# A Perceiver-like stack on one core: how the two mixtures of experts open, and where their router products and block list are made

## The reference, cut to what matters

```
x += cross attention over 8192 context rows, padded by a mask      (L0x)
x += self attention, keys j >= i only                              (L0a)
x += mixture: 8 experts, hidden size 2048, silu, top 2             (L0f)
x += cross attention over the context, masked by rows and columns  (L1x)
x += self attention in a window of 64 keys                         (L1a)
x += mixture: 8 experts, hidden size 1024, relu squared, top 2     (L1f)
```

```python
logits = xf @ router
top_v, top_i = jax.lax.top_k(logits, TOP_K)
w = jax.nn.softmax(top_v, axis=-1)
gates = jnp.sum(jax.nn.one_hot(top_i, E, dtype=x.dtype) * w[..., None], axis=1)
for e in range(E):
    h = xf @ W1[e]
    h = h * jax.nn.sigmoid(h)
    out = out + gates[:, e:e + 1] * (h @ W2[e])
```

## Time and profile before

| | us |
|---|---|
| median of 3 runs | 1856.64 (1856.35 to 1856.89) |
| profiled execution | 1861.01 |
| its span, first to last instruction | 1859.2 |
| TensorE busy | 1628.2 (88%) |
| VectorE busy | 1025.4 (55%) |
| ScalarE busy | 529.0 (28%) |
| GpSimd busy | 99.2 (5%) |
| mean granted clock of TensorE | 0.928 |

### The profile page before, as it was taken

How to read it: one execution, slowest core, us unless ns; L and a number is a source line. 1 busy time by engine, 2 the same in 40 slices (tenths; PEclk the granted TensorE clock), 3 DMA queues, 4 the chain that set the end, 5 groups by cost and what they waited for, 6 DMA issues and landing times. The chain is left out here.

```text
span 1859.2 us, 27460 instructions
## 1 busy us (share of the span) xinstructions
PE 1628.2 (88%) x9315; PEld 748.2 (40%) x9327; DVE 1025.4 (55%) x1655; ACT 529.0 (28%) x775; POOL 99.2 (5%) x82
## 2 busy tenths in 40 slices
PE   4899997999898949999999699997899898849994
PEld 1333322222233347765565233332222234447773
DVE  3577766999745521111111589996799735522222
ACT  1333423788413301111111111113578312200000
POOL 0100000200001010000001200002000001010001
PEclk9999978999998959999999799988999998969997
DMA  3424443221046367666661312315221020048995
GB/s 134 157 81 154 159 152 117 75 58 34 0 142 120 52 269 262 237 237 221 236 231 47 118 65 106 113 45 187 59 80 34 0 80 30 32 161 323 320 331 171
DMA packets 81010, 252.36 MB, mean 136 GB/s; under 512 B 7808, under 2 KB 25232, under 8 KB 60976
## 3 DMA queue, kind: packets, MB, share of 16 engines
q1 hardware_dynamic: 75120, 237.33, 38.2%
q0 software_dynamic: 2560, 8.39, 1.4%
q10 hardware_dynamic: 3264, 5.77, 0.8%
HBM read 223.68 MB, written 38.27 MB: 141 GB/s over the span
## 5 line engine op out<-in xcount | busy, mean ns | idle before, releaser
L1375 ACT ACTIVATE BIG<-banks 128x1024 f32<-128x1024 f32 (+5 forms) x320 | 282.0, 933 | 123.8 <-PE banks L1310 123.8
L937 DVE CUSTOM_DVE_ANT_0 BIG<-banks,MASK,MX 128x512 bf16<-128x512 f32 (+5 forms) x384 | 229.2, 656 | 75.8 <-PE banks L604 38.1
L1763 PEld LDWEIGHTS banks<-KF,BIG 128*128 128x128 f32 x1792 | 231.7, 194 | 13.7 <-issue 13.7
L1763 PE MATMUL banks<-KF,BIG 128*128 128x160 f32 (+1 forms) x1792 | 233.9, 293 | 2.0 <-DVE KF L1586 2.0
L604 PE MATMUL banks<-KF,XN 32*128 32x512 f32 (+4 forms) x1280 | 200.8, 635 | 18.8 <-DVE MX L937 9.4
L1780 PE MATMUL banks<-BIG,PB 128*128 128x512 f32 x448 | 202.8, 600 | 0.0
L1307 PE MATMUL banks<-XN,KF 32*128 32x512 f32 (+4 forms) x1280 | 174.2, 615 | 23.3 <-ACT BIG L1375 7.8
L1425 DVE TENSOR_TENSOR PB<-PB,BIG 128x2048 f32<-128x2048 f32 (+5 forms) x78 | 166.9, 2139 | 33.9 <-ACT BIG L1375 29.6
L930 DVE TENSOR_REDUCE MXW<-banks 128x2 f32<-128x1024 f32 x128 | 150.4, 1217 | 55.5 <-PE banks L615 54.7
L579 PE MATMUL banks<-WV,XNT 128*128 128x512 f32 x320 | 164.6, 636 | 0.0
L1277 PE MATMUL banks<-BIG,V 128*32 128x512 f32 (+4 forms) x1280 | 159.9, 568 | 2.9 <-ACT BIG L1375 2.8
(11 more groups left out here) (259 smaller groups left out, 1416.8 us busy)
## 6 DMA issues: line engine op xcount, KB each, us to landing
BIG<-in_L0f_w SPq DMA_DIRECT2D x64, 1024.0 KB, 4.7
BIG<-in_L1f_w SPq DMA_DIRECT2D x48, 1024.0 KB, 5.4
BIG<-in_mask_q SPq DMA_DIRECT2D x16, 1024.0 KB, 9.1
CT<-in_ctx SPq DMA_DIRECT2D x9, 1024.0 KB, 4.8
XNT<-in_ctx SPq DMA_DIRECT2D x9, 1024.0 KB, 5.9
k_saved<-KF SPq DMA_DIRECT2D x32, 256.0 KB, 2.7
v_saved<-V SPq DMA_DIRECT2D x32, 256.0 KB, 2.4
KF<-k_saved SPq DMA_DIRECT2D x32, 256.0 KB, 3.4
```

The source lines that it names most:

```text
L937: last = v.tensor_tensor_reduce(m.JUNK[:, 2 * half + e, k0:k1], pair[:, e, k0:k1], bias, 1.0, mx, ALU.add, ALU.max, mx)
L1375: a.activation(m.PE_[:, s % NP, 2 * half:2 * half + 2, q0:q1], m.pair[(2 * s + half) % 3][:, :, q0:q1], ACT.Exp).then_inc(exp_ready, 1)
L1763: last = t.matmul(out, W1[k][:, d, f * P:(f + 1) * P], XE[:, d, :], start=d == 0, stop=d == DC - 1)
```

## The change

- `project_out` of the two self attentions makes the router's logits itself, tile by tile, in bank 5: `logits(q)` stands after the output products of tile q + 2, the last two after the transposes of tiles 2 and 3. The mixture no longer makes them.
- Ranks: four products instead of ten. One covers the four tiles with the triangular weights, three add the earlier tiles to all later ones at once (the moving operand is repeated).
- Rows of rounds 0 and 1: VectorE makes a one-hot matrix HOT (tokens by slots, RS columns for each of four tiles) for experts 0 and 1 by comparing the rank with a ramp; TensorE multiplies XN by it (`hot_rows`), 16 products each, straight into the banks where the transposes would put them. Round 0's come right after the ranks, round 1's in round 0 in place of the transposes. HBM is read from round 2 on. The constant `rows` moves next to `ramp` so that the ramp can be 160 wide.
- The loads of rows move from SyncE to ScalarE, where they stand between the activations and the output copy of a round, under a conditional, behind a wait for the whole scatter and one for the transposes.
- TensorE's loop body has two conditionals more, `If(i < 1)` and `If(i >= 1)`. The number of rounds is written earlier (`counted`), and TensorE and ScalarE wait for that instead of the full list.
- The block list of L1x moves into the `row_maxima` of L0a: on TensorE after the first keys and queries, before the first scores, with a wait for its end; on VectorE ahead of the maxima.

```diff
@@ class Attention / row_maxima
+    U = unmasked_blocks(nc, m, n + "_blocks", m.UNMASKED[:, :, :], L.lists) if L.lists is not None else None
             if not dyn:
                 all_keys(0, [0])
                 all_queries(0)
+                if U:
+                    U.tensor(pe)
+                    pe.wait_ge(U.listed, U.listed_at)
                 pe.wait_ge(wv_loaded, 16)
                 scores(0, False)
...
             if not dyn:
                 dve.wait_ge(steps_done, 2)
+                if U:
+                    U.vector(dve)
                 maxima(0, False)
@@ project_out, tensor
+            def logits(q):
+                if router_loaded is None:
+                    return
+                pe.wait_ge(copied, q + 1)
+                for d in range(DC):
+                    last = t.matmul(m.bank[OUT[0]][:, E * q:E * q + E], m.XNT[:, d, q * P:(q + 1) * P], m.WR[:, d, :],
+                                    start=d == 0, stop=d == DC - 1)
+                last.then_inc(logits_done, 1)
...
                 last.then_inc(output_ready, 1)
+                if q > 1:
+                    logits(q - 2)
                 if q:
                     turn(q - 1)
+            logits(NQ - 2)
             turn(NQ - 1)
+            logits(NQ - 1)
@@ mixture, vector
-            dve.wait_ge(products_done, 1)
-            do(v.tensor_copy(LG, m.bank[0][:, 0:32]))
+            do(v.tensor_copy(LG, m.bank[5][:, 0:32]))
...
+            def one_hot(e):
+                for q in range(NQ):
+                    do(v.tensor_scalar(HOT[:, e, q, :], m.wide_ramp[:, 0:RS], RK[:, E * q + e:E * q + e + 1],
+                                       SM[:, E * q + e:E * q + e + 1], ALU.is_equal, ALU.mult))
+            one_hot(0)
+            m.mark["hot"] = m.steps
+            dve.wait_ge(products_done, 2)
+            do(v.tensor_scalar(m.CTL[0:1, C_NR:C_NR + 1], m.bank[3][0:1, 16:17], float(E), None, ALU.add))
+            m.mark["counted"] = m.steps
             do(v.tensor_scalar(CU, m.bank[3][0:E, 0:1], float(E), None, ALU.add))
             do(v.tensor_scalar(LE, m.ramp[0:E, 0:16], CU, None, ALU.is_ge))
             m.mark["of_round"] = m.steps
+            one_hot(1)
+            m.mark["hot1"] = m.steps
...
             m.mark["slots"] = m.steps
+            dve.wait_ge(transposed, 1 + B)
+            v.tensor_copy(XE[:, :, :].rearrange("p (a c) n -> p a (c n)", a=2), tokens).then_inc(tokens_copied, 1)
@@ mixture, sync: load_rows and its waits removed; the loads for L1x stand right behind W2
@@ mixture, scalar, after the activations of a round
+                    with act.If(i + 1 < nr):
+                        act.wait_ge(scattered, 2 * NQ * 16)
+                        wait_alone(act, transposed, i + 2 + B)
+                        act.dma_start(ROWS, XS[bass.ds(at + 2, 1), 0:P, :]...).then_inc(rows_loaded, 16)
@@ mixture, tensor
+            t.matmul(m.bank[7][:, 0:NQ * E], m.before[:, :], SM, start=True, stop=False, skip_group_check=True)
+            for b in range(NQ - 1):
+                last = t.matmul(m.bank[7][:, E * (b + 1):NQ * E].rearrange("p (t e) -> p t e", e=E), m.ones[:, :],
+                                r3(SM)[:, b:b + 1, :].to_broadcast([P, NQ - 1 - b, E]), start=False, stop=b == NQ - 2,
+                                skip_group_check=True)
...
+            def hot_rows(e):
+                for d in range(DC):
+                    out = tokens[:, d // 2, (d % 2) * RS:(d % 2) * RS + RS]
+                    for q in range(NQ):
+                        last = t.matmul(out, m.XN[:, q, d * P:(d + 1) * P], HOT[:, e, q, :], start=q == 0, stop=q == NQ - 1)
+                last.then_inc(transposed, 1)
+            pe.wait_ge(steps_done, m.mark["hot"])
+            hot_rows(0)
...
-                    transposes(i + 1)
+                    with pe.If(i < 1):
+                        pe.wait_ge(steps_done, m.mark["hot1"])
+                        hot_rows(1)
+                    with pe.If(i >= 1):
+                        transposes(i + 1)
```

93 lines of the change are left out of this document (39 added, 54 removed).

## The result

The changed kernel takes 1835.7 us (median of 4 runs, 1831.1 to 1837.0), the kernel before in the same comparison 1856.7 (1856.35 to 1856.89): ratio 0.988, 95% interval 0.9865 to 0.990, about 21 us faster. Forecast were 1823.2 us in a range of 1817 to 1832. The sign was right; of the 33.4 us forecast some 12 did not come. There the kernel before itself spread from 1849.6 to 1863.8 us in 23 runs, so a few microseconds between two medians of six runs say little, and what follows goes by the places in the traces as much as by the times.

What follows compares the result with a forecast made beforehand. TensorE was taken to bound the rounds, one serial path through several engines and DMA the mixtures' openings. Mixtures -22.4 and -20.8, attention ends +5.6, list +4.2 made -33.4 us: 1856.6 to 1823.2 us, range 1817 to 1832.

Steps and rivals of the forecast that it cites:

- Openings: Both mixtures, start to first hidden product: 16.05 us against 38.2 (-22.1) and 16.0 against 37.6 (-21.6).
- Clock in round 0 and rows of round 1: Mixtures: round 0 at high clock -2.9 and -2.3 us; round 1's row products on TensorE's path +2.6 and +3.1.
- Mixtures as a whole: Opening, round 0 clock and round 1 rows summed: first mixture -22.4 us, second -20.8.
- Ends of the attentions: Logits between output products end each windowed attention 2.4 to 3.6 us later; 2.8 taken twice, +5.6.
- List: Block list ahead of the second attention's first scores: +4.2 us (3.5 to 5.5), some 2 more if the clock falls.
- A: Mixtures' round 0: clock not risen after the row products, low clock paid twice, up to 5.2 us, 1828.4; chance 0.15.
- B: TensorE's loop: two more conditionals in each of 20 rounds, exposed, cost 4.6 us, 1827.8; chance 0.10.
- D: First mixture: W1 and W2 mixed in the queue, first W1 about 5 us late for the row products, 1828; chance 0.03.
- C: TensorE's loop: instructions fetched anew after jumping over row products, 2.5 us in 20 rounds, +50 us, 1873; chance 0.03.

Runs made afterwards that it cites:

- list_between: Changed kernel with the block list's four groups of TensorE products spread between the projections' products: 1835.1 us, ratio 0.988.
- two padded kernels: Kernel before with 19, changed kernel with 18 unread 8-column products at layer 1's start: 1862.8 us (ratio 1.004) and 1834.9 us (0.988).
- two paused ones: Changed kernel and kernel before, each with three extra VectorE statistics at layer 1's start: 1842.2 us (ratio 0.993) and 1859.6 us (1.002).
- filled: Changed kernel with list products spread and unread 256-column products in gaps at attention ends, selections, values' starts and layer 1's start: 1817.0 us, ratio 0.978.
- warm_half: Changed kernel with unread 256-column TensorE products added at the windowed attentions' ends and in each mixture's selection: 1834.5 us, ratio 0.989.

## Why the prediction was wrong, point by point

- **Openings: right.** 22.1 and 21.6 us were to go; from the stage's start to the first hidden product it went from 39.6 to 17.6 (mean of two) and from 38.5 to 17.9, so 21.9 and 20.7. The one-hots took 1.56 instead of 1.25 us, the row products 7.11 and 5.51 instead of 6.9 and 5.2. That they came within 0.9 us is due to rows of the same shapes in the old trace.
- **Clock in round 0 and rows of round 1: right in the first, 0.4 off in the second.** The first round with its rows took 41.4 us where 41.5 less 0.3 was the sum, the second's 17.7 where 16.5 plus 0.8 was.
- **Mixtures as a whole:** -21.4 and -19.4 instead of -22.4 and -20.8. The first mixture of the kernel before was 1.0 us shorter in its second trace; I had taken my rows from the longer one.
- **Ends of the attentions: right place, too small.** +5.6 was taken, +8.0 measured. The estimate had 2.4 at the full and 3.6 at the low clock. The first end gave 3.0 and 4.8 us, the longer one with the clock low for its last 6.9 us; the second gave 4.2 in both traces.
- **List: +4.2 taken, +4.9 measured,** inside the bounds of 3.5 to 5.5, but not by the forecast's sum: the list's own delay is 3.5, and the rest comes from the clock falling behind it, which the forecast had outside its 4.2. `list_between` shows that 3.4 can be covered: its low stretch behind the list is gone as well.
- **The step that failed** is the one that was not written down: that stages without an edit keep their time, a term put at nothing. Of the 14.2 us that are missing in the traces (33.4 less 19.2) the terms above make 5.5 (mixtures 2.4, ends 2.4, list 0.7); stages without an edit make 8.7. 4.4 of these are in L1x's values: 3.2 to 3.7 are the standstill behind the loop, shown by the two padded kernels with the two paused ones beside them. The rest of the 4.4 is not separated; the clock's low stretch around the standstill is 6.8 us instead of 3.4 in the traces that have it. 3.6 are in L0a's values' part, where the clock was low for longer (`filled` removes it), the cause not shown and changing between executions of the same code. The rest, -1.5 to +1.6 us a stage, is no more than two traces of one kernel differ by.
- **The rivals.** A, B and D did not happen: round 0 began at the full clock, no gap stands around the conditionals, and the first hidden products waited for VectorE's copy only. C named the right mechanism at the wrong place: TensorE does wait for instructions, but not at each jump over the row products. It was priced at 2.5 us in each of 20 rounds; it comes once, behind another stage's loop, at 3.2 to 3.7 us. Round 0 lost time only in variants, up to 3.0 us in the first mixture and 4.3 in the second; both traces of the changed kernel have none of it. In the second mixture these idle times are put down to "issue", in the first mostly to VectorE, and their cause is open. Rival C should have been asked what else the moved code does, not only how often the new jump is taken.
- **The range** ended at 1832. Its width held the unknown terms and no term for the clock and the code of everything else.

## What to carry to other kernels

An edit that adds or moves instructions moves all code behind it on that engine: where a loop or a jump is left, look for idle time put down to issue together with transfers of the instruction queue, and test with a few harmless instructions ahead before you blame or praise the edit. A term moved out of a chain is worth its length only if nothing else stands beside the chain: here taking 7 us of logits out of the first opening brought 2.7 us while the rows waited for busy transfers, and 6.7 once they did not. Where TensorE stands idle ahead of its work, cheap products in the gap can be worth more than shortening the work, as long as they end before the wait does: filling 4.8 us in L0a's values made that part 6.5 us shorter than the mean of the changed kernel's two traces.

## What was not expected of the hardware

- The same code with 76 instructions more ahead of it stood still for 6.4 us instead of 1.8 at one place; with a delay of the same size and no such instructions it stood for 1.8.
- Round 0 of the first mixture took 44.4 instead of 41.4 us in the kernel whose only edit is three VectorE operations that run after it; the traces don't tell why.
- 6.96 us of logit products without a gap left the clock at 0.50. With products of 256 columns in the waits at the attention's end and in the selection, the opening of `warm_half` stood at 0.89. Which of the two places did it is not separated.
- A kernel's own runs differ by 6 to 14 us with nothing changed (0.945 of granted clock goes with 1830.1 us, 0.938 with 1839.5 in the changed kernel), and four runs of the kernel before that lay within 0.6 us did not show it.
